# Turning two weight blocks on VectorE instead of TensorE in a two-layer cross-attention

## What is computed

```
x: (4, 1024, 1024)   ctx: (4, 64, 1024)
# layer 0: 32 query heads, 8 key heads, head size 32, mask added, Wq Wk Wv Wo with biases
out = softmax(q k^T * scale + mask) v;  x = layer_norm(out @ Wo + bo + x) * gamma + beta
# layer 1: 16 heads of 64
a = layer_norm(ctx, ln_gamma, ln_beta)
Q = x @ Wq.T;  K = a @ Wk.T;  V = a @ Wv.T
out = softmax(mask(Q K^T * scale)) V @ Wo.T
result = x + tanh(gate) * out
```

## Time and profile before

| | |
|---|---|
| median of three runs | 1812.03 us (1809.41 to 1812.71) |
| profiled execution, in all | 1808.57 us |
| its span | 1806.8 us |
| PE busy | 1737.9 us, 96% |
| DVE, ACT, POOL busy | 1090.4, 582.8, 1104.6 us |
| granted PE clock, mean | 0.99 |

### The profile page before, as it was taken

The page is one execution under the profiler, slowest core; times in us unless marked ns, Lnnn a source line. Parts: engine busy times, 40 slices in busy tenths (PEclk is TensorE's granted clock), DMA queues, the critical chain, the costliest instruction groups (busy, mean ns, idle before and its releaser), DMA issues.

```text
span 1806.8 us, 22550 instructions
## 1 busy us (share of the span) xinstructions
PE 1737.9 (96%) x8576; PEld 1445.9 (80%) x8576; DVE 1090.4 (60%) x1070; ACT 582.8 (32%) x666; POOL 1104.6 (61%) x610
## 2 busy tenths in 40 slices
PE   5999999999999899999999988899999999999998
PEld 4788888888888688888888867788888888888887
DVE  6888888888879444444444453646644664466442
ACT  3444444444445433333333322213311331133110
POOL 3577777777789856565655585536543664466431
PEclk9999999999999899999999989899999999999999
DMA  9433332332326556666667844454845474556332
GB/s 215 107 80 76 85 79 73 88 80 72 75 80 175 171 184 236 207 240 212 233 227 233 291 138 141 140 171 132 256 130 173 130 224 147 163 161 189 124 121 94
DMA packets 273515, 278.02 MB, mean 154 GB/s; under 512 B 64512, under 2 KB 224384, under 8 KB 273408
## 3 DMA queue, kind: packets, MB, share of 16 engines
q1 hardware_dynamic: 272256, 275.53, 49.3%
q10 hardware_dynamic: 1152, 1.05, 0.3%
HBM read 174.77 MB, written 101.71 MB: 153 GB/s over the span
## 4 chain that ended last, share of the span: by engine, by line
PE 64%; DVE 16%; issue 8%; ACT 5%; POOL 3%; DMA 2%; SPq 1%; DVEq 0%; ACTq 0%
PE ps L53 20%; PE ps L55 20%; PE ps L54 20%; DVE small L1023 4%; DVE pr L1046 4%; ACT pr L795 3%; DVE pT0r L1057 2%; DVE pT1r L1057 2%; DVE xT0r L953 2%; ACT ot L789 2%; DVE xT1r L953 2%; PE ps L657 1%; PE ps L665 1%; PE ps L632 1%; POOL oc1l L1276 1%
## 5 line engine op out<-in xcount | busy, mean ns | idle before, releaser
L1324 POOL TENSOR_TENSOR x2Tl<-x2r,x2Th 128x1024 fp32r<-128x1024 f32 x32 | 76.9, 2403 | 292.1 <-ACT x2Th L896 292.1
L1130 DVE STREAM_TRANSPOSE x2r<-xd 128x1024 f32<-128x1024 f32 x32 | 68.7, 2147 | 207.9 <-PE ps L55 207.9
L1264 POOL TENSOR_TENSOR pr<-pr,small 128x1024 f32<-128x1024 f32 x64 | 121.9, 1905 | 99.8 <-DVE small L1052 99.8
L896 ACT CAST x2Th<-x2r 128x1024 fp32r<-128x1024 f32 x32 | 33.7, 1052 | 375.9 <-DVE x2r L1130 375.9
L1259 POOL TENSOR_TENSOR pr<-pr,small 128x1024 f32<-128x1024 f32 x64 | 123.9, 1936 | 20.9 <-DVE small L1027 20.9
L1023 DVE TENSOR_REDUCE small<-pr 128x16 f32<-128x1024 f32 x64 | 78.1, 1220 | 78.2 <-ACT pr L795 78.2
L1281 POOL TENSOR_TENSOR xb<-xb,bo 128x1024 f32<-128x1024 f32 x32 | 78.6, 2455 | 73.6 <-DMA xb<-in_x_dram 73.6
L1295 POOL TENSOR_TENSOR y<-y,bet 128x1024 f32<-128x1024 f32 x32 | 76.8, 2399 | 74.8 <-DVE y L1069 74.8
L1100 DVE TENSOR_TENSOR y<-ps,xb 128x512 f32<-128x512 f32 x64 | 44.0, 688 | 114.1 <-PE ps L55 111.2
L53 PE MATMUL ps<-wo0h,oc0l 128*128 128x512 f32 x256 | 104.4, 408 | 5.5 <-DVE wo0l L977 3.0
L53 PE MATMUL ps<-wo0h,oc1l 128*128 128x512 f32 x256 | 103.1, 403 | 5.7 <-DVE y L1100 5.7
(11 more groups left out here) (368 smaller groups left out, 5503.3 us busy)
## 6 DMA issues: line engine op xcount, KB each, us to landing
o_scratch<-ot SPq DMA_DIRECT2D x256, 64.0 KB, 1.8
ocr<-o_scratch SPq DMA_DIRECT2D x16, 1024.0 KB, 7.4
xb<-in_x_dram SPq DMA_DIRECT2D x32, 512.0 KB, 6.7
x_scratch<-y SPq DMA_DIRECT2D x32, 512.0 KB, 5.2
a_scratch<-ost SPq DMA_DIRECT2D x64, 256.0 KB, 3.5
b_scratch<-ost SPq DMA_DIRECT2D x64, 256.0 KB, 5.0
xd<-x_scratch SPq DMA_DIRECT2D x128, 128.0 KB, 2.9
raw<-b_scratch SPq DMA_DIRECT2D x64, 256.0 KB, 5.9
```

What stands on the lines that cost most here:

```text
L1264: nc.gpsimd.tensor_tensor(heads(v), heads(v), mx.unsqueeze(2).to_broadcast([P, TPB * GRP, KEYS]), ALU.subtract)\
L1324: nc.gpsimd.tensor_tensor(x2T[1][:], x2r[:], f32(x2T[0][:]), ALU.subtract).then_inc(x2_lo, 1)
```

## The change

Wk1 and Wv1 are no longer turned by PE. Their loads lay the block out in four groups of partitions, four transfers for each matrix instead of one, and DVE turns it with one block transpose of 128x1024 into a new buffer `wTr` in SBUF (`turn_wt`, at the end of its program for the slot of step 0 or 1). ACT's cast and DVE's subtraction read `wTr` instead of PSUM. Since this turn puts feature 8p + k on partition p of block k, the context has to be in that order too: `turn_norm` reads every eighth column, and gamma1 and beta1 are loaded as dense rows of eight values. PE's wait for the last evacuations of the round before goes from step 0 to step 2, where `TT` is now first written.

```diff
-        wt = [at(f"wt{i}", 56 + 4 * i, [P, D]) for i in range(2)]
+        wt = [at(f"wt{i}", 56 + 4 * i, [P, TPB, D // TPB]) for i in range(2)]
+        wTr = at("wTr", 200, [P, KT, P])
...
-                sp.dma_start(dst, w[name].rearrange("(k p) -> p k", p=P), allow_slow_non_contiguous=True).then_inc(n_ld, 16)
+                sp.dma_start(dst, w[name].rearrange("(p k) -> p k", k=KT)).then_inc(n_ld, 16)
...
-                    sp.dma_start(wt[i][:], w[name][P * f:P * (f + 1), :]).then_inc(wt_ld[i], 16)
+                    for a in range(4):
+                        sp.dma_start(wt[i][32 * a:32 * (a + 1)], w[name][P * f:P * (f + 1), 256 * a:256 * (a + 1)]
+                                     .rearrange("(t j) c -> j t c", t=TPB)).then_inc(wt_ld[i], 16)
...
-                                                   ctxn[:, r, HALF * i + P * k:HALF * i + P * (k + 1)], ident[:])
+                                                   ctxn[:, r].rearrange("p (c e) -> p c e", e=KT)[:, :, 4 * i + k], ident[:])
...
             def table_part(f, s):
-                if s in (0, 1):
-                    if s == 1:
-                        project(pe, f, 0)
-                    pe.wait_ge(wt_ld[s], 16 * (f + 1))
-                    if s == 0:
-                        if f == 0:
-                            pe.wait_ge(n_raw, 2)
-                        after(pe, evac_a, 8 * f)
-                        after(pe, evac_d, 8 * f)
-                    else:
-                        pe.wait_ge(wT_lo, 2 * f + 1)
-                    for k in range(KT):
-                        last = nc.tensor.transpose(TT[:, P * k:P * (k + 1)], wt[s][:, P * k:P * (k + 1)], ident[:])
-                    last.then_inc(wt_turned, 1)
+                if s == 0:
+                    return
+                if s == 1:
+                    project(pe, f, 0)
                 elif s == 2:
                     project(pe, f, 1)
                     pe.wait_ge(w1_ld[1], 16 * (f + 1))
+                    after(pe, evac_a, 8 * f)
+                    after(pe, evac_d, 8 * f)
...
-                        nc.scalar.copy(wT[0][:], TT).then_inc(wT_hi, 1)
+                        nc.scalar.copy(wT[0][:], wTr[:]).then_inc(wT_hi, 1)
...
-                        nc.vector.tensor_tensor(wT[1][:], TT.rearrange("p (k c) -> p k c", k=KT), f32(wT[0][:]),
-                                                ALU.subtract).then_inc(wT_lo, 1)
+                        nc.vector.tensor_tensor(wT[1][:], wTr[:], f32(wT[0][:]), ALU.subtract).then_inc(wT_lo, 1)
...
                 f, s = table(h)
+                if f is not None and s in (0, 1):
+                    turn_wt(f, s)
...
+            def turn_wt(f, i):
+                if f == 0 and i == 0:
+                    dve.wait_ge(n_turned, 2)
+                    dve.wait_ge(o_st[0], 64 * UNITS // 2)
+                dve.wait_ge(wt_ld[i], 64 * (f + 1))
+                after(dve, wT_lo, 2 * f + i)
+                nc.vector.transpose(wTr[:].rearrange("p k (t j) -> p t k j", t=TPB),
+                                    wt[i][:].rearrange("p t (i k) -> p t k i", k=KT)).then_inc(wt_turned, 1)
```

## The result

| | before | changed |
|---|---|---|
| median of the runs made side by side | 1811.05 us (4 runs) | 1830.24 us (4 runs, 1828.86 to 1833.98) |
| ratio, 95% interval | 1 | 1.0112, 1.010 to 1.0125 |
| profiled execution / span | 1808.57 / 1806.8 us | 1830.51 / 1828.7 us |

The change makes the kernel slower by 19.2 us in the medians, 21.9 us between the two profiled executions. 1827.4 us was forecast.

The account below looks back on a forecast made before the run. PE was taken to bound the table stage. Chain losses less gains +6.0, clock loss +8.6 and strided reads +0.8 made +15.4 us on the median of 1812.03: 1827.4 us, own range 1823 to 1832, 8 in 10 1816 to 1836.

Parts of the forecast that it names:

- PE loses 16 x 0.87 us: Table stage: PE drops 16 groups of eight weight transposes, 13.9 us, the whole possible gain.
- Odd rounds: the chain of Wk1 grows by 3.28 us behind a late gamma: Ahead of project(f, 0): DVE's transpose, ACT's cast and handovers add 3.28 us; rounds 3, 5, 7 lose 9.84, round 1 3.04.
- The stalls: 3.9 and 3 x 4.3 us: Ahead of project(f, 0): PE sits idle 3.9 us in round 1 and about 4.3 us in the other odd rounds.
- rival C: Table stage: each two-SBUF subtraction meets a POOL operation, up to 2.15 us each, 7.2 us more, 1834.6 us; chance 0.12.
- Even rounds: +0.6 us of wait, gain 0.18: Rounds 2, 4, 6: PE waits 0.6 us ahead of project(f, 0), yet each gains 0.18 us, 0.54 in all.
- Round 0: loss 0.66: Project start of round 0 moves from 640.04 to 640.70, a loss of 0.66 us, with a 1.5 us wait.
- Wv1 hidden, -7.0 us: All rounds: turning Wv1 takes 6.1 us against 8.4 available, so it is hidden and 7.0 us are won.
- Clock: 4 x 2.15 = 8.6 us: Behind the four odd-round stalls PE's clock falls, costing 2.15 us each, 8.6 in all; ends 6.8 and 10.4.
- Strided reads +0.8 (0 to 1.7): PE's 16 transposes of ctxn read every eighth float: 0.8 us more, bounds 0 and 1.7.
- Loads and dense gamma1, beta1: 0: Wk1 and Wv1 in 8 pieces instead of 2, and dense gamma1 and beta1 loads, cost nothing.
- A (no clock loss): Table stage: stalls come but PE's clock holds or barely falls, +6.8 us, 1819 us; chance 0.15.
- B (the late link): Odd rounds: if the affine came 3 us earlier against PE, every round is like the even ones, 1804.4 us; chance 0.08.

Follow-up runs that it names:

- best version: Changed kernel with Wk1's transpose, cast and subtraction early and POOL's coefficients ahead of its chunk halves: 1791.40 us, ratio 0.9901.
- coefficients first: Changed kernel with POOL's four coefficient operations ahead of its two chunk halves: everywhere 1803.23 us, only up to the end of the table stage 1805.27 us.
- filled run: Changed kernel with 38 more matmuls, their result unread, on PE ahead of project(f, 0) in rounds 1, 3, 5 and 7: 1822.78 us, ratio 1.0066.
- early turn: Changed kernel with only Wk1's transpose on DVE one slot earlier, cast and subtraction left in place: 1813.62 us, ratio 1.0019.

## Why the prediction was right

Its forecast (1827.4) was 2.8 us low, inside its own range, and its mechanism is what the runs show. That the number came so close is in part luck: it had added +15.4 us, where the medians differ by 19.2 and the profiled executions by 21.9, and it started from a median of three runs that a fourth brought down by 1.0 us. By its steps:

- *PE loses 16 x 0.87 us.* Right, and by PE's own pace a group is worth 0.90 us: where PE does not wait, 8.34 us from project to project instead of 9.24. The best version got the whole sum back.
- *Odd rounds: the chain of Wk1 grows by 3.28 us behind a late gamma.* The mechanism is right and shown from both sides: take the chain away (transpose, cast and subtraction early) or take the lateness away (coefficients first), and the stalls go. The size of the chain was good: from gamma to project in round 3, 780.54 to 784.32 plus 3.28 is 7.06 us, and 793.98 - 786.81 = 7.17 was measured.
- *The stalls: 3.9 and 3 x 4.3 us.* Too small; 4.93, 5.41, 4.96, 5.99 were measured, 21.3 against 16.8. Two things were missed. First, gamma came later against PE, by 0.9 us in round 1 and 1.0 in round 3 (0.2 and 0.3 in rounds 5 and 7). In round 3 it had started 3.64 us ahead of the end of PE's half tile (2.77 with the 0.87 taken off), and in the changed kernel 1.76. The prediction had held that this link "moves with PE" because PE's work releases the transfer. The issue does; the transfer does not keep its length. From issue to POOL's start it was 9.34 and 9.74 us in rounds 1 and 3 of the changed kernel, 8.56 and 8.29 before; the run with only Wv1 moved shows the same in round 3. What made it longer was not tested. Second, the subtraction now at the end of the chain took 1.47, 1.46, 1.85 and 2.96 us in odd rounds, not 1.21; that is 2.9 us, all of it on the path, and rival C's mechanism in part, at 2.9 instead of 7.2 us.
- *Even rounds: +0.6 us of wait, gain 0.18.* Right: 0.65, 0.65 and 0.64 us of wait.
- *Round 0: loss 0.66.* Its stall was 2.16 us, not 1.5, and behind it the clock fell (0.90, then 0.67), which the prediction had put at 0: 1.5 us. Yet project(f, 0) started at 639.91, 0.1 us ahead of before, since PE had come to that place sooner.
- *Wv1 hidden, -7.0 us.* Hidden, yes, but the 7.0 us are won only in rounds whose chain is not late. The run with Wv1 alone got 2.7 us of them in its stretch. The prediction had added the two terms as if each stood alone.
- *Clock: 4 x 2.15 = 8.6 us.* The filled run confirms the mechanism (7.5 us). In the odd rounds it was 1.4 to 1.9 each, 6.5 in all, just under the lower end of 6.8; round 0 brings it to 8.0.
- *Strided reads +0.8 (0 to 1.7).* Probably too high: 0.6 us (-0.9 to +2.4) for all of them with 16 more strided groups, which is nothing that stands out of the noise. The doubling that a strided cast on ACT showed does not carry over to PE. The Trainium skill, "SBUF — State Buffer", section on the DMA port swizzle, note on cachelines, puts a penalty on such reads; the trace agrees in sign alone, with 0.02 to 0.04 us on 0.90.
- *Loads and dense gamma1, beta1: 0.* Right; SP's wait in that place is 137.1 us against 149.2, and no wait of PE came from it.

Against the 13.9 us that the prediction has for this stretch (5.3 without round 0, and 8.6 of clock), the 5.7 us that are missing are idle time ahead of project(f, 0) +4.6, waits for bd1l and in project(f, 1) +1.1, clock -0.6, and 0.6 unaccounted for. Of the signs that it named, rounds 2 to 3 came out 5.45 us longer (96.31 to 101.76) instead of 3.5, and the low part ran above 2 us in 5 of 16 cases, one of them ahead of a project(f, 0).

Of the rivals, A (no clock loss) fell with the filled run and B (the late link) named the right switch. Its price was -8.4 us in the table; the kernel with coefficients first there measured 337.69 against 346.03, -8.34, with the six waits of about 0.7 us that it had for even rounds. Its sum for the chain held too: in round 3 of the run with the coefficients first everywhere the turning started at 777.03, 3.35 us ahead of the end of PE's half tile at 780.38; the 4.59 us that the prediction has from turning to project (2.15 + 0.04 + 1.05 + 0.04 + 1.21 + 0.10) leave a stall of 1.24, and 1.24 was measured. The prediction names the chunk halves as part of the lateness, but asks only whether the transfer could be shorter. With the transfer no shorter (9.97 us from issue to POOL's start in that round), it was enough that these 4.7 us and the coefficients change places.

## What to carry to other kernels

Moving work off the bounding engine is worth its full time only where the chain into its next instruction has slack; here the odd rounds had none, and the same move cost 19.6 us or won 13.5 in the table stretch, by the place of one block's transpose, cast and subtraction and the order of two pieces of POOL's work. When a chain is lengthened, first ask what starts it and whether anything not urgent is queued ahead of that on its engine. A stall of the matrix engine is to be priced with the clock behind it: here 6.5 us on top of 21.3 us of stall in the odd rounds, though single stalls lost from nothing to half their length and more.

## What the runs showed of the hardware

- **The clock behind short stalls is not a matter of length alone.** Loss is here what project(f, 0) to project(f, 1) takes more than in the same kernel's quiet rounds. The four stalls of 4.93 to 5.99 us in the changed kernel lost 1.4 to 1.9 us; with only Wk1 moved, 4.70 lost 2.3 and 5.36 lost 2.1; with the coefficients first, 4.71 lost 2.4. With the early turn 2.12, 2.68 and 3.05 us lost 1.5 each. Stalls of 1.69, 1.81 and 1.92 us lost nothing. But 2.16 us in round 0 of the changed kernel (clock 0.90 and 0.67 in the two stretches of four microseconds) cost 1.5, while 2.20 us at the same place with only Wk1 moved cost nothing. Why was not found:

```profile
638.00:642.00 4.00, 1.96 (x14) 1.53 (x13) 3.12 (x3) 4.00 (x4) 2.71 (x2) 1.00 0.22 91
642.00:646.00 4.00, 4.00 (x30) 3.77 (x30) 0.74 (x3) 2.06 (x3) 4.00 (x2) 1.00 0.38 135
```

- **A subtraction of two SBUF tensors waits for POOL; a block transpose does not.** This subtraction took from 1.21 to 5.45 us in these runs. Where a POOL instruction had 0.3 us or more left to run when it began (75 of 128 in the nine profiles that have it) it took 1.4 us or more, elsewhere 1.21 to 1.28. POOL's work grows as well where it comes second: an operation on 128x1 at 0.12 us behind the subtraction's start took 1.16 us, where it takes 0.19 alone (897.2 us in the filled run). The block transposes of the changed kernel, with POOL busy beside them as at 789.28 us, stayed within 2.02 and 2.19, and no other run has one above 2.28. The Trainium skill, "SBUF — State Buffer", Who interferes with whom, has the port that the two share as an exclusive lock. The rows above agree: POOL's residual add ends at 878.45, 1.22 us of subtraction on top would give 879.67, and it ended at 879.53.
- **A float32 block transpose of 128x1024 takes 2.07 us on VectorE in the median**; eight 128x128 transposes are worth 0.90 us of TensorE's time when they read densely (9.24 less 8.34), and 0.92 to 0.94 when they read every eighth float.
